# A gated cross-attention and a 2:4 sparse feed-forward layer: mask as a product, merged GpSimd operations, a rewritten order of the first steps

## The reference

```
xn  = layernorm(x)
a   = softmax(mask ? xn @ ctx.T / sqrt(512) : -1e30)        # 128 x 128 for each row
x1  = x + tanh(g_xattn) * valid * (a @ ctx)
n   = layernorm(x1)
h   = silu(n @ w_gate) * (n @ w_up)                         # 2048 wide
h   = of every 4 neighbours in h the 2 largest by magnitude, the others 0
out = x1 + tanh(g_ffn) * (h @ w_down)
```

## Time and profile before

| | us |
|---|---|
| median of three runs | 1132.81 |
| profiled execution | 1133.86 |
| its span | 1132.10 |
| TensorE busy | 1083.6 (96%) |
| VectorE busy | 811.0 (72%) |
| ScalarE busy | 620.8 (55%) |
| GpSimd busy | 198.8 (18%) |

### The profile page before, as it was taken

How to read it: one execution, slowest core, us unless ns; L and a number is a source line. 1 busy time by engine, 2 the same in 40 slices (tenths; PEclk the granted TensorE clock), 3 DMA queues, 4 the chain that set the end, 5 groups by cost and what they waited for, 6 DMA issues and landing times.

```text
span 1132.1 us, 15204 instructions
## 1 busy us (share of the span) xinstructions
PE 1083.6 (96%) x4960; PEld 882.1 (78%) x4960; DVE 811.0 (72%) x1421; ACT 620.8 (55%) x1132; POOL 198.8 (18%) x393
## 2 busy tenths in 40 slices
PE   6988897899998999999999999999999999999998
PEld 5867575687786888888888888888888888888886
DVE  6999858879696676657675757475756666575766
ACT  6989665576766454444454545455545444444552
POOL 5777400110111111111100100111111111111001
PEclk9999999999999999999999999999999999999999
DMA  7999475798897977788789777887878666767726
GB/s 260 332 331 326 165 278 178 229 308 260 270 274 220 374 220 195 189 235 219 184 233 351 209 203 204 210 255 188 229 224 275 157 154 153 195 151 200 195 31 137
DMA packets 92350, 254.76 MB, mean 225 GB/s; under 512 B 9072, under 2 KB 9072, under 8 KB 87920
## 3 DMA queue, kind: packets, MB, share of 16 engines
q1 hardware_dynamic: 74416, 221.28, 56.1%
q0 software_dynamic: 17856, 32.51, 21.8%
HBM read 154.14 MB, written 99.61 MB: 224 GB/s over the span
## 4 chain that ended last, share of the span: by engine, by line
PE 74%; DVE 18%; issue 3%; DMA 3%; ACT 1%; SPq 1%; DVEq 0%; POOL 0%; ACTq 0%
PE ps_a L1135 9%; PE ps_a L1139 9%; PE ps_a L1137 9%; PE ps_y L1206 9%; PE ps_y L1208 9%; PE ps_y L1207 9%; PE ps_d L1135 4%; PE ps_d L1137 4%; PE ps_d L1139 4%; PE ps_c L1135 2%; PE ps_c L1139 2%; PE ps_c L1137 2%; DMA x_blk<-xnT_scratch 2%; DVE bn L875 2%; DVE beats L925 2%
## 5 line engine op out<-in xcount | busy, mean ns | idle before, releaser
L558 POOL DMA_DIRECT2D out_rows<-y_out x124 | 107.2, 866 | 875.5 <-ACT y_out L687 850.6
L1135 PE MATMUL ps_a<-xm,w_ring 128*128 128x512 f32 x512 | 202.1, 395 | 10.5 <-ACT cp L637 5.5
L1137 PE MATMUL ps_a<-xm,w_ring 128*128 128x512 f32 x512 | 201.7, 394 | 0.0
L1139 PE MATMUL ps_a<-xm,w_ring 128*128 128x512 f32 x512 | 201.6, 394 | 0.0
L1206 PE MATMUL ps_y<-dn,h_hi 128*128 128x512 f32 x480 | 189.8, 395 | 12.2 <-ACT y_out L687 12.1
L1208 PE MATMUL ps_y<-dn,h_lo 128*128 128x512 f32 x480 | 187.8, 391 | 0.0
L1207 PE MATMUL ps_y<-dn,h_hi 128*128 128x512 f32 x480 | 187.4, 390 | 0.0
L687 ACT ACTIVATE y_out<-ps_y,ffn_gate 128x512 f32<-128x512 f32 x124 | 85.1, 686 | 147.8 <-PE ps_y L1208 147.7
L893 DVE TENSOR_TENSOR cp<-ps_c,cp 128x512 f32<-128x512 f32 x64 | 43.9, 690 | 142.5 <-PE ps_c L1139 142.5
L667 ACT ACTIVATE h_hi<-hidden 128x512 fp32r<-128x512 f32 x128 | 73.1, 624 | 98.5 <-DVE hidden L951 98.5
L1135 PEld LDWEIGHTS ps_a<-xm,w_ring 128*128 128x128 f32 x512 | 97.3, 190 | 32.2 <-issue 8.7
(11 more groups left out here) (105 smaller groups left out, 1858.8 us busy)
## 6 DMA issues: line engine op xcount, KB each, us to landing
w_ring<-w_scratch SPq DMA_DIRECT2D x147, 512.0 KB, 4.3
out_rows<-y_out POOLq DMA_DIRECT2D x124, 256.0 KB, 4.3
w_scratch<-w_ring SPq DMA_DIRECT2D x56, 512.0 KB, 5.3
xm_scratch<-x_out SPq DMA_DIRECT2D x42, 512.0 KB, 5.0
xm<-xm_scratch SPq DMA_DIRECT2D x21, 1024.0 KB, 7.3
w_raw<-in_L_ffn_w_down SPq DMA_DIRECT2D x9, 1024.0 KB, 7.9
x_in<-in_x SPq DMA_DIRECT2D x32, 256.0 KB, 5.0
ctx_in<-in_ctx SPq DMA_DIRECT2D x32, 256.0 KB, 5.2
```

Of the source, the lines that this page charges most:

```text
L558: nc.gpsimd.dma_start(out[RING * (n // (2 * TILES * QS)) + TILES * ORDER[order] + n % TILES], y_out[:, n % 4], accum_op=ALU.add).then_inc( ...
L1135: nc.tensor.matmul(to, w_ring[:, k, e, 0, c], xm[:, k, 0, c], start=begins and c == 0, stop=False, skip_group_check=not begins)
L1137: nc.tensor.matmul(to, w_ring[:, k, e, 0, c], xm[:, k, 1, c], start=False, stop=False, skip_group_check=not begins)
L1139: last = nc.tensor.matmul(to, w_ring[:, k, e, 1, c], xm[:, k, 0, c], start=False, stop=c == 1, skip_group_check=not begins)
```

## The change

Four things change.

1. *Scores.* ScalarE's copy of the transposed ctx multiplies by -scale. TensorE adds the mask as a fifth product of one row: ones (1 x 128) times `mask_neg` (1 x 128). VectorE's `neg_scores` is gone, the minimum and the exponential read PSUM.
2. *GpSimd.* The first norm of row n+1, the second norm of row n-6 and the softmax sum of row n-4 lie side by side; one add and one power do what three powers and two adds did. `out_scale` is gone: the gate is multiplied in by ScalarE when it copies the transposed probabilities. VectorE computes the first statistics a slot earlier.
3. *Inputs.* Nine instead of eight rows are loaded ahead (`INPUTS`).
4. *Order.* In step 0 and the start of step 1 the lists of SP, ScalarE and VectorE are new: unit 2's weights and the low parts of the down weights are built earlier, `x_blk` is loaded in slot 36. In steps 1 to 3 the spreads 0 and 1 of unit u+1 stand between the two copies of ps_a.

The diff, cut to its core (buffers, semaphores and the renaming of `RING` to `INPUTS` left out):

```diff
+        if n == SLOTS - 3:
+            load_x_blk(sp, 1, 0)
+
+    load_w_piece(sp, 2, 2)
+    for k in range(5):
+        store_w(1, k)
     load_dn(0)
-    for s in range(STEPS):
+    store_w(1, 5)
+    x_stored_at(0, 0)
+    load_w_piece(sp, 2, 3)
+    store_w(1, 6)
+    load_w_piece(sp, 3, 0)
+    store_w(2, 0)
+    store_w(2, 1)
+    x_stored_at(0, 1)
+    load_w_piece(sp, 3, 1)
+    for k in range(2, 6):
+        store_w(2, k)
+    x_stored_at(0, 2)
+    store_w(2, 6)
+    x_stored_at(0, 3)
+    for s in range(1, STEPS):
...
+    for n in range(-1, SLOTS - 1):
+        k = n % RING
+        first, second, third = n + 1 < B, 0 <= n - 6 < B, 0 <= n - 4 < B
+        if first:
+            pool.wait_ge(stats1_done, n + 2)
+        if second:
+            pool.wait_ge(stats2_done, n - 5)
+        if first or second:
+            part_v = slice(0 if first else 1, 2 if second else 1)
+            nc.gpsimd.tensor_tensor(base3[:, k, part_v], bn_mv[:, k, part_v, 1], eps[:, part_v],
+                                    ALU.add).then_inc(base_done, 1)
+            pool.wait_ge(base_done, n + 2)
+        if first:
+            nc.gpsimd.tensor_tensor(neg_mean[:, k:k + 1], bn_mv[:, k, 0, 0:1], minus_one[:],
                                     ALU.mult).then_inc(neg_mean_done, 1)
-        pool.wait_ge(var_eps_done[which], b + 1)
-        nc.gpsimd.tensor_tensor(rstd[:, which, k:k + 1], var_eps[:, which, k:k + 1], minus_half[:],
-                                ALU.pow).then_inc(rstd_done[which], 1)
-
-    for n in range(SLOTS):
-        if 0 <= n - 6 < B:
-            inverse_deviation(1, n - 6)
-        if n < B:
-            inverse_deviation(0, n)
-            k = n % RING
-            pool.wait_ge(neg_mean_done, n + 1)
-            pool.wait_ge(rstd_done[0], n + 1)
-            nc.gpsimd.tensor_tensor(neg_mean_rstd[:, k:k + 1], neg_mean[:, k:k + 1], rstd[:, 0, k:k + 1],
+        if third:
+            pool.wait_ge(probs_done, n - 3)
+        part_p = slice(0 if first else 1, 3 if third else 2 if second else 1)
+        nc.gpsimd.tensor_tensor(power3[:, k, part_p], base3[:, k, part_p], exponent3[:, part_p],
+                                ALU.pow).then_inc(power_done, 1)
...
+            nc.scalar.activation(ctxT[:, b % 2], ps_cT, ACT.Copy, scale=-SCALE).then_inc(cT_copied, 1)
...
+            nc.scalar.activation(probs[:, b % 2], ps_sc[b % 2][:, 0:M], ACT.Exp, bias=neg_max[:, b % RING:b % RING + 1],
+                                 scale=-1.0, accum_out=base3[:, (b + 4) % RING, 2:3]).then_inc(probs_done, 1)
...
         if s > 0:
             absolute(s - 1, 1, 0)
             copy_a0(u, 0)
+            if building:
+                spread(act, u + 1, 0)
             absolute(s - 1, 1, 1)
             copy_a0(u, 1)
+            if building:
+                spread(act, u + 1, 1)
             absolute(s - 1, 1, 2)
             absolute(s - 1, 1, 3)
-            for j in tiles:
-                h_high(s - 1, 0, j)
-            silu0(u, 0)
-            silu0(u, 1)
-            copy_a1(u, 0)
-            copy_a1(u, 1)
+            if s == 1:
+                silu0(u, 0)
+                silu0(u, 1)
+                copy_a1(u, 0)
+                copy_a1(u, 1)
...
+            silu0(0, 0)
+            silu0(0, 1)
+            copy_a1(0, 0)
+            copy_a1(0, 1)
             w_high(act, 1, 2)
-            copy_d0(u, 0)
-            copy_d0(u, 1)
+            copy_d0(0, 0)
+            copy_d0(0, 1)
             w_high(act, 1, 3)
+            spread(act, 2, 0)
+            w_high(act, 1, 4)
+            silu1(0, 0)
+            silu1(0, 1)
+            w_high(act, 1, 5)
 
             for k in range(4):
                 act.wait_ge(x1_stored[k], 16 * (B // 4))
             for k in range(2):
                 act.wait_ge(xnT_stored[k], 16 * (PAIRS - 1))
-            x_high_at(s, 0)
-            silu1(u, 0)
-            silu1(u, 1)
-            for k in range(4, PROD):
-                w_high(act, 1, k)
-            x_high_at(s, 1)
+            x_high_at(0, 0)
+            w_high(act, 1, 6)
+            spread(act, 2, 1)
+            copy_a0(1, 0)
+            spread(act, 2, 2)
+            copy_a0(1, 1)
+            for j in first:
+                absolute(0, 0, j)
+            w_high(act, 2, 0)
+            silu0(1, 0)
+            silu0(1, 1)
+            w_high(act, 2, 1)
+            copy_a1(1, 0)
+            copy_a1(1, 1)
+            x_high_at(0, 1)
+            spread(act, 2, 3)
+            copy_d0(1, 0)
+            copy_d0(1, 1)
+            w_high(act, 2, 2)
+            w_high(act, 2, 3)
+            for j in range(GROUP):
+                dn_high(0, j)
+            w_high(act, 2, 4)
+            silu1(1, 0)
+            silu1(1, 1)
+            w_high(act, 2, 5)
+            x_high_at(0, 2)
+            for j in second:
+                absolute(0, 0, j)
+            w_high(act, 2, 6)
+            x_high_at(0, 3)
+            continue
...
         b = n - 3
         if 0 <= b < B:
-            wait(dve, probs_done, b - 1)
             dve.wait_ge(scores_done, b + 1)
-            if b % RING == 0:
-                dve.wait_ge(mask_neg_done, b // RING + 1)
-            nc.vector.scalar_tensor_tensor(neg_scores[:, b % 2], ps_sc[b % 2][:, 0:M], -SCALE,
-                                           mask_neg[:, b * M:b * M + M], ALU.mult, ALU.add).then_inc(neg_scores_done, 1)
-            dve.wait_ge(neg_scores_done, b + 1)
-            nc.vector.tensor_reduce(neg_max[:, b % RING:b % RING + 1], neg_scores[:, b % 2], AX.X,
+            nc.vector.tensor_reduce(neg_max[:, b % RING:b % RING + 1], ps_sc[b % 2][:, 0:M], AX.X,
                                     ALU.min).then_inc(neg_max_done, 1)
         b = n - 5
         if 0 <= b < B:
-            dve.wait_ge(out_scale_done, b + 1)
+            dve.wait_ge(power_done, n + 1)
             dve.wait_ge(av_done, b + 1)
             wait(dve, x1_stored[b % 4], 16 * (b // 4))
-            nc.vector.scalar_tensor_tensor(x1[:, b % 4], ps_av[b % 2][:], out_scale[:, b % RING:b % RING + 1],
-                                           x_in[:, b % RING], ALU.mult, ALU.add).then_inc(x1_done, 1)
+            nc.vector.scalar_tensor_tensor(x1[:, b % 4], ps_av[b % 2][:], power3[:, (n - 1) % RING, 2:3],
+                                           x_in[:, b % INPUTS], ALU.mult, ALU.add).then_inc(x1_done, 1)
         b = n - 6
         if 0 <= b < B:
             wait(dve, nT_done, b - 1)
...
+            dve.wait_ge(power_done, n + 2)
+            nc.vector.tensor_scalar(x1n[:, b % 2], x1[:, b % 4], bn_mv[:, n % RING, 1, 0:1],
+                                    power3[:, n % RING, 1:2], ALU.subtract, ALU.mult).then_inc(x1n_done, 1)
...
+        elif s == 1:
+            for j in tiles:
+                h_low(0, 0, j)
+            compare(0, 1, first + second)
+            add_c22(u, 0)
+            add_c22(u, 1)
+            compare(0, 1, REST)
+            add_c12(u, 0)
+            add_c12(u, 1)
+            x_low_at(s, 0)
+            count_wins(0, 1)
+            keep(0, 1, tiles[:2])
+            for j in tiles[:2]:
+                h_low(0, 1, j)
...
+            add_c11(0, 0)
+            add_c11(0, 1)
             w_low(dve, nc.vector, 1, 0)
             w_sum(dve, 1, 2)
             w_low(dve, nc.vector, 1, 1)
             w_sum(dve, 1, 3)
             w_low(dve, nc.vector, 1, 2)
-            add_c22(u, 0)
-            add_c22(u, 1)
+            add_c22(0, 0)
+            add_c22(0, 1)
             w_low(dve, nc.vector, 1, 3)
-            x_low_at(s, 0)
-            add_c12(u, 0)
-            add_c12(u, 1)
             w_low(dve, nc.vector, 1, 4)
-            gated0(u, 0)
-            gated1(u, 0)
-            gated0(u, 1)
-            gated1(u, 1)
+            add_c12(0, 0)
+            add_c12(0, 1)
+            gated0(0, 0)
             w_low(dve, nc.vector, 1, 5)
+            gated0(0, 1)
+            gated1(0, 0)
+            gated1(0, 1)
+            x_low_at(0, 0)
             w_low(dve, nc.vector, 1, 6)
-        x_low_at(s, 1)
+            add_c11(1, 0)
+            add_c11(1, 1)
+            w_low(dve, nc.vector, 2, 0)
+            compare(0, 0, first)
+            w_low(dve, nc.vector, 2, 1)
+            x_low_at(0, 1)
+            for i in range(4):
+                w_sum(dve, 2, i)
+            add_c22(1, 0)
+            add_c22(1, 1)
+            w_low(dve, nc.vector, 2, 2)
+            w_low(dve, nc.vector, 2, 3)
+            dn_low(0)
+            add_c12(1, 0)
+            add_c12(1, 1)
+            w_low(dve, nc.vector, 2, 4)
+            gated0(1, 0)
+            w_low(dve, nc.vector, 2, 5)
+            gated0(1, 1)
+            gated1(1, 0)
+            gated1(1, 1)
+            x_low_at(0, 2)
+            compare(0, 0, REST + second)
+            w_low(dve, nc.vector, 2, 6)
+            add_c11(2, 0)
+            add_c11(2, 1)
+            count_wins(0, 0)
+            keep(0, 0, kept_order(0))
+            x_low_at(0, 3)
+            continue
...
```

(34 more changed lines are left out.)

186 lines of the change are left out of this document (82 added, 104 removed).

## The result

The changed kernel takes 1145.59 us, median of 4 runs (1145.36 to 1146.48), against 1133.21 us beside it: a ratio of 1.0103, 95% interval 1.0085 to 1.0121. It is slower. The forecast was 1134.5, the range 1122 to 1149; the case that I gave 0.37 is not what came, though the time lies in the range. The profiled executions have spans of 1144.2 and 1132.1 us, so 12.1 us are to be found.

The account below looks back on a forecast made before the run. VectorE was taken to bound attention, waits the early feed-forward, TensorE from about 360 us on. Attention +6.0, steps 0 and 1 -6.3, steps 2 and 3 +2.0 summed to +1.7 us: 1134.5 us on the median, range 1122 to 1149.

Parts of the forecast that it names:

- the case that I gave 0.37: Whole kernel: the forecast itself, +1.7 us, 1134.5 us on the median, own range 1129 to 1140; chance 0.37.
- The bound and the path: Attention: VectorE bounds; x1n waits for GpSimd's add, neg_mean and power, 1.33 us from the second aggregate against 1.26.
- the first rival: Attention: GpSimd answers before VectorE reaches x1n, so 0.30 us count in 14 slots; -10.4 us, 1122.4 us; chance 0.24.
- The price of a column: GpSimd's merged power in attention: each further column costs 0.05 us, range 0.001 to 0.36.
- the prediction's formula: Attention slot: grows by 0.08 us plus two further power columns, 0.18 us in all; +4.5 us over 25 slots.
- the second rival: Attention: each column of the power costs 0.36 us, slot grows by 0.80; +18.4 us, 1151.2 us; chance 0.27.
- The start: Attention start: a ninth input pair ahead of the first weight piece delays ScalarE; +1.8 us, between 0 and 2.5.
- Steps 0 and 1: Feed-forward: the rewritten order fills VectorE's idle time, so the end of down(0, 0) comes earlier; -6.3 us.
- The walk: Feed-forward steps 0 and 1: new queues followed operation by operation; VectorE waits 9.1 us, 7.7 less; down(0, 0) ends 7.6 earlier.
- the prediction's two cases: Unit 2's last raw weight piece lands at 164 us, or at 167 with 5.0 us saved; the middle, -6.3, was taken.
- the third rival: Feed-forward: the weight piece lands at 171 us or later, losing or halving 6.3 us; +4 to +8, about 1139; chance 0.12.
- Steps 2 and 3: Feed-forward: moved spreads stall ScalarE, so h_low starts 1.0 us later in each step; +2.0 us, bounds 0 and +2.6.

Follow-up runs that it names:

- e1: Changed kernel with the second norm's add and one-column power parted from the merged operations, on their own semaphores; 1134.57 us, ratio 1.0008.
- e11: Changed kernel without the mask's product, so scores are unmasked; 1144.75 us, ratio 1.0095.
- e8: e1 without the mask's product, so scores are unmasked; 1131.41 us, ratio 0.9978.
- e2: Changed kernel with GpSimd's one power of a slot over six columns instead of three, the further three unused; 1159.38 us, ratio 1.0222.
- e9: Changed kernel with 8 input buffers instead of 9, nothing else; 1143.92 us, ratio 1.0082.
- e4: Kernel before with the change's order edits alone, its attention and 8 inputs kept; 1135.12 us, ratio 1.0016.
- e12: e4 with the spreads of steps 2 and 3 at their former place and unit 2's last weight piece behind three stores; 1125.90 us, ratio 0.9940.
- e6: Changed kernel with the edits of e1 and e3, and unit 2's last weight piece issued behind three weight stores instead of six; 1124.11 us, ratio 0.9919.
- e3: Changed kernel with ScalarE's weight spreads of steps 2 and 3 back at their former place, step 1's left moved; 1140.34 us, ratio 1.0061.

## Where the prediction held and where it failed

**The bound and the path: right.** I wrote that what x1n waits for sets the slot, that it would wait for the power in nearly every slot, and that the 0.30 us of `neg_scores` would be lost again. It waits for the power in all slots but the first, 0.62 us in 22 of 32 and 18.2 us in all; taking most of this wait away (e1) gives 11.0 us back, and leaving out the mask's product (e11) gives only 0.8. The three pieces of the path that the trace of before could show are right to 0.01 us. One floor was set too low: with the mask's product a slot of TensorE takes 3.48 us (e1) and not near 3.2, since that product costs 0.31 (e8) where I allowed 0.27 at most; the first rival would have gained less than I gave it.

**The price of a column: the step that failed first.** I took 0.05 us for a further column, "nearer to the conversion, which shows that this engine's loop over columns is short". It is 0.15 (e2 holds it to six columns). A power's loop over columns isn't that of a conversion or an add: of the 0.55 us of a one-column power 0.40 are fixed and 0.15 the column. With 0.15 the prediction's formula gives 0.08 + 0.30 = 0.38 per slot, which is what was measured, and 9.5 over its 25 slots, where the loop measures +8.9 and I had +4.5. My bounds, 0.001 and 0.36, held it, and "slower begins at 0.12" named the point that it passed: between the forecast and the second rival. The choice inside the bounds lacked a reason from a row of a power. By the rule of the Trainium skill (GPSIMD Engine Reference, 3.1 Elementwise) that I weighed, a further column would have been free. For the add the trace agrees (192 to 197 ns); for the power it does not.

**The start: the size fits, the cause doesn't.** +1.8 was put down to the ninth pair of inputs. The first x1n is 1.55 us later, but stays there with 8 buffers (e9). Without the mask's product it is at 26.72 (e11), so 0.6 of it may be that product: TensorE waits 2.38 us for the first `mask_neg` at 13.90. e4 and e12, whose attention is the kernel before's, have 25.94 and 27.76, e12 with a granted clock of 0.79 from 24 to 30 us. The runs don't settle what moves the start.

**Steps 0 and 1: -4.7 for -6.3.** The walk held, in both of its cases. Without a stall it has `down(0, 0)` start 64.8 us after unit 0 and end 7.6 earlier than before; e6, where the piece is early, has 64.5 and 8.1. With the piece late it saves 5.0; the changed kernel saves 4.7. The piece landed at 176.7, 34.2 us after unit 0's start, where the prediction's two cases are 31.8 and 34.8, and VectorE stood 5.02 us for it. So the later case came, and the middle of the two was the mis-sized term; the third rival, a landing at 171 or later (38.8), did not come. From issue to landing it took 10.8 us instead of the 7.3 of the earlier trace rows, because stores and the down weights stood ahead of it: e6 takes them away, and `down(0, 0)` ends 2.8 us earlier. One sum is off: the waits that the walk lists add up to 9.9 us, not 9.1, which would leave 7.0 saved. That e6 still fits is in part luck.

**Steps 2 and 3: +6.4 for +2.0, the second step that failed.** The delay was right: h_low 1.01 us late, the last tile of each down product 1.1 us late, 2.2 for my 2.0. What I put at nothing was TensorE's clock. The other 4.2 us are products at a lower granted clock: 2.4 in the last tile of `down(1, 0)` (5.28 us for 2.86), 0.4 in the products behind it, 1.4 in the last tile of `down(2, 0)` (4.29 for 2.86). My upper bound, +2.6, had no place for them. e3 shows that they go with the spreads' place; why the clock falls there stays open.

**The sum.** The three terms are +4.3, +1.6 and +4.4 off, which is, but for 0.1, the distance between +1.7 and 12.1. With 0.15 us a column and all else as it stood the prediction would have said about +6.7 us (25 x 0.38 + 1.8 - 0.3 - 6.3 + 2.0). That the time fell inside the range is owed to the bounds kept for the column, which happened to cover the clock's 4.2 us as well. The chances slip too: 0.24 and 0.03 are both taken from a rival given 0.24, and the cases as they stand leave 0.37 for "slower", which came, not 0.34.

## What to carry to other kernels

Merging small operations of one engine saves that engine's time and lengthens the wait of whoever needs the first of the results: count it from the consumer that is the bound, and give that consumer's part its own instruction and semaphore. A price per element is taken from the same operation or kept open between its bounds, since an add and a power differ by 30 times in it. When an instruction that waits is moved up a queue, the delay that it brings to the next bound is one term, and TensorE's granted clock behind the gap is another: look at it tile by tile, and note whether a wait behind a slow tile takes the loss up. What is issued to a DMA queue ahead of an urgent load counts as much as when that load is issued.

## What the runs showed of the hardware

GpSimd's power costs 0.40 us and 0.15 per column of 128 partitions (556, 698, 852, 1167 and 1323 ns for 1, 2, 3, 5 and 6 columns), the add 192 and 197 ns for 1 and 2.

A small operation of GpSimd that is under way while VectorE makes x1n can end only when x1n has ended. In e1 the two-column power at 47.45 takes 0.95 us and ends at 48.40, 0.03 behind x1n; the one at 56.01, behind x1n's main part, takes 0.69. neg_mean takes 0.19 us at 47.31 and 0.46 at 55.60, inside x1n, ending 0.04 behind it. (Not always: in the changed kernel neg_mean_rstd, begun at 48.93, 0.03 ahead of x1n, takes its usual 0.19.)

```profile
47.31 0.19 POOL L551 TENSOR_TENSOR neg_mean<-bn_mv,minus_one 128x1 f32<-128x1 f32 x1
47.45 0.95 POOL L557 TENSOR_TENSOR power<-base,exponent 128x2 f32<-128x2 f32 x1
...
55.60 0.46 POOL L551 TENSOR_TENSOR neg_mean<-bn_mv,minus_one 128x1 f32<-128x1 f32 x1
56.01 0.69 POOL L557 TENSOR_TENSOR power<-base,exponent 128x2 f32<-128x2 f32 x1
```

```profile
47.83 0.54 DVE L914 TENSOR_SCALAR x1n<-x,bn_mv,power 128x512 f32<-128x512 f32 x1
...
55.47 0.55 DVE L914 TENSOR_SCALAR x1n<-x,bn_mv,power 128x512 f32<-128x512 f32 x1
```

No run was made for this alone.

Twelve products of a down tile take 2.86 us at a granted clock of 1.00, 4.44 at 0.62 and 5.28 at 0.50. TensorE had waited 1.39 us, worked 3.0 and waited 2.9 ahead of the slow ones (e4, after) and ahead of a fast one (e12), so these waits alone don't decide it.
